# Attention's products cut into four products of 32 weight columns

## What is computed

```
Q = x @ Wq.T + bq ; K = x @ Wk.T + bk ; V = x @ Wv.T + bv      (heads of 8)
scores = einsum(Q, K) / sqrt(128), causal ; attn = softmax(scores)
x = layernorm(x + attn @ V @ Wo.T + bo)
w, i = top 2 of softmax(x @ gate_w.T), weights renormalised
x = layernorm(clip(x + w0 * expert_i0(x) + w1 * expert_i1(x)))
expert(x) = gelu(x @ w1 + b1) @ w2 + b2                        (128 -> 256 -> 128)
```

## Time and profile before

| what | value |
|---|---|
| median of 3 runs | 498.77 us (498.0 to 500.38) |
| profiled execution, span | 529.2 us |
| PE / weight loads / DVE / ACT / POOL busy | 84% / 53% / 74% / 62% / 52% |
| attention of one batch, steady | 40.3 us (from 142.3 to 182.6 us of the span) |
| in it: PE / DVE / ACT busy | 38.3 / 36.8 / 28.6 us |

### The profile page before, as it was taken

How to read it: one execution, slowest core, us unless ns; L and a number is a source line. 1 busy time by engine, 2 the same in 40 slices (tenths; PEclk the granted TensorE clock), 3 DMA queues, 4 the chain that set the end, 5 groups by cost and what they waited for, 6 DMA issues and landing times.

```text
span 529.2 us, 11188 instructions
## 1 busy us (share of the span) xinstructions
PE 442.3 (84%) x3577; PEld 279.2 (53%) x3610; DVE 389.1 (74%) x979; ACT 328.7 (62%) x810; POOL 275.6 (52%) x443
## 2 busy tenths in 40 slices
PE   8799999999999999999999898685687867776980
PEld 2355454454454454454454453264586866675970
DVE  7978889988989989989989998558444544442192
ACT  5285766776777776776776667456265766565045
POOL 6033234266456456456546557826655655656363
PEclk9999999999999999999999999989578898989896
DMA  6646595552542542452542311232333322221463
GB/s 179 194 150 185 162 279 162 159 152 82 169 152 83 171 151 77 147 178 77 159 138 87 102 52 30 74 83 78 103 108 97 82 71 69 69 63 32 144 215 119
DMA packets 74393, 64.60 MB, mean 122 GB/s; under 512 B 9030, under 2 KB 68685, under 8 KB 74336
## 3 DMA queue, kind: packets, MB, share of 16 engines
q1 hardware_dynamic: 68240, 55.01, 35.3%
q0 software_dynamic: 4512, 8.54, 5.0%
q10 hardware_dynamic: 1584, 0.34, 0.3%
HBM read 36.88 MB, written 25.46 MB: 118 GB/s over the span
## 4 chain that ended last, share of the span: by engine, by line
PE 47%; DVE 26%; issue 8%; ACT 7%; another core or an unknown queue 5%; DMA 3%; POOL 2%; ACTq 0%; SPq 0%; DVEq 0%; POOLq 0%
DVE nmax L1354 15%; PE psum L1022 9%; PE psum L1189 8%; PE psum L998 7%; PE psum L975 6%; PE psum L1206 6%; PE psum L983 3%; DMA experts<-o_dram 2%; DVE ov L1362 2%; PE psum L1043 2%; PE psum L1050 2%; PE psum L1181 2%; ACT probs L806 2%; PE psum L1082 1%
## 5 line engine op out<-in xcount | busy, mean ns | idle before, releaser
L806 ACT ACTIVATE probs<-psum 128x512 f32<-128x512 f32 x320 | 180.2, 596 | 85.2 <-PE psum L998 45.6
L1354 DVE TENSOR_REDUCE nmax<-psum 128x2 f32<-128x1024 f32 (+3 forms) x224 | 196.3, 911 | 23.7 <-PE psum L983 23.2
L689 POOL TENSOR_SCALAR_AFFINE_SELECT probs<-probs 128x512 f32<-128x512 f32 x186 | 85.0, 484 | 125.6 <-ACT probs L806 124.9
L975 PE MATMUL psum<-kst,qst 128*128 128x512 bf16 (+2 forms) x511 | 109.6, 300 | 6.4 <-DVE nmax L1354 5.6
L757 POOL DMA_INDIRECT o_dram<-probs,xs x77 | 76.8, 997 | 59.0 <-DVE probs L1583 34.0
L998 PE MATMUL psum<-qst,kst 128*128 128x128 bf16 (+3 forms) x480 | 102.0, 296 | 6.5 <-issue 2.9
L1022 PE MATMUL psum<-probs,vst 128*32 128x512 f32 (+3 forms) x1024 | 83.1, 442 | 0.1
L983 PE MATMUL psum<-bmask,bident 128*128 128x256 bf16 (+1 forms) x320 | 80.5, 251 | 0.1
L998 PEld LDWEIGHTS psum<-qst,kst 128*128 128x128 bf16 x512 | 40.4, 98 | 54.6 <-ACT probs L806 32.1
L975 PEld LDWEIGHTS psum<-kst,qst 128*128 128x128 bf16 x512 | 47.1, 98 | 32.9 <-DVE nmax L1354 12.3
L1189 PE MATMUL psum<-xsT,kst 128*128 128x128 f32 x148 | 27.3, 314 | 17.5 <-ACT hT_sb L919 11.5
(11 more groups left out here) (217 smaller groups left out, 709.8 us busy)
## 6 DMA issues: line engine op xcount, KB each, us to landing
kst<-dk SPq DMA_DIRECT2D x62, 128.0 KB, 3.0
qst<-dq SPq DMA_DIRECT2D x31, 256.0 KB, 3.1
xs<-xs_dram SPq DMA_DIRECT2D x77, 66.0 KB
experts<-o_dram SPq DMA_DIRECT2D x7, 512.0 KB, 4.4
dk<-k SPq DMA_DIRECT2D x7, 384.0 KB, 2.7
dq<-q SPq DMA_DIRECT2D x7, 384.0 KB
xT_sb<-in_xT SPq DMA_DIRECT2D x8, 256.0 KB
xTv_sb<-in_xT SPq DMA_DIRECT2D x8, 256.0 KB, 3.4
```

The source lines that it names most:

```text
L689: pool.affine_select(out=view, in_=view, compare_op=ALU.is_ge, fill=0.0, base=0, pattern=[[0, view.shape[1]], [1, P]], channel_multiplier= ...
L806: act.activation(probs[:, c % 2, p, kk * T:(kk + 1) * T], ps_t[:, k % 2, :], ACT.Exp, scale=SCALE).then_inc(S["exp_done"], 1)
L975: pe.matmul(bank[:, at:at + w], qst[:, c, e, P * i:P * i + P], kst[:, c, h, e, 0:w], start=(at == 0), stop=False, skip_group_check=True)
L1354: last = dve.tensor_reduce(o, i, AX.X, ALU.max, negate=True)
```

## The change

A helper `columns` issues a product as four narrow ones, each with 32 of the weight columns and 32 partitions of the output, with the same moving operand. It is used for the scores and their masks, the values, the output product and the ranks, and, from batch 1 on, for the projections and what is taken off them (`whole_or_columns`). The turning of the maxima becomes a single narrow product, since only 32 of the 128 columns of `nmq` were ever filled; `nmq` shrinks to 32 columns, and its clearing on DVE at the start goes. The ranks were one product with `tri` and ten of 14 columns with `ones`; now each of the four tiles of `hotb` is repeated over all the blocks behind it by a moving operand of stride 0, so that there are four products with `ones` (56, 42, 28 and 14 columns) beside that with `tri`, each of them cut in four.

```
-        nmq = sb("nmq", [P, 2, P], BF16)
+        nmq = sb("nmq", [P, 2, 32], BF16)
...
+            def columns(out, stationary, moving, **flags):
+
+                for g in range(4):
+                    last = pe.matmul(out[32 * g:32 * g + 32], stationary[:, 32 * g:32 * g + 32], moving,
+                                     skip_group_check=True, **flags)
+                return last
+
+            def whole_or_columns(b, out, stationary, moving, start):
+
+                if b == 0:
+                    return pe.matmul(out, stationary, moving, start=start, stop=True, skip_group_check=True)
+                return columns(out, stationary, moving, start=start, stop=True)
...
-                        pe.matmul(bank[:, at:at + w], qst[:, c, e, P * i:P * i + P], kst[:, c, h, e, 0:w],
-                                  start=(at == 0), stop=False, skip_group_check=True)
+                        columns(bank[:, at:at + w], qst[:, c, e, P * i:P * i + P], kst[:, c, h, e, 0:w],
+                                start=(at == 0), stop=False)
...
-                            last = pe.matmul(ps_t[:, k % 2, at % T:at % T + w],
-                                             kst[:, c, g % 2, pair, P * j:P * j + P],
-                                             qst[:, c, pair, P * j:T], start=True, stop=True, skip_group_check=True)
+                            last = columns(ps_t[:, k % 2, at % T:at % T + w],
+                                           kst[:, c, g % 2, pair, P * j:P * j + P],
+                                           qst[:, c, pair, P * j:T], start=True, stop=True)
...
-                pe.matmul(ps_o[:, 0:P], nmq[:, c % 2, :], bident[:], start=True,
+                pe.matmul(ps_o[0:32, 0:P], nmq[:, c % 2, :], bident[:], start=True,
...
-                        last = pe.matmul(halves[:, n, :], onT_sb[:, P * i:P * i + P], wo_sb[:], start=True, stop=True)
+                        last = columns(halves[:, n, :], onT_sb[:, P * i:P * i + P], wo_sb[:], start=True, stop=True)
...
-                    pe.matmul(ps_m[:, 0:EB], tri[:], hotb[:].rearrange("p i e -> p (i e)"), start=True, stop=False,
-                              skip_group_check=True)
+                    columns(ps_m[:, 0:EB], tri[:], hotb[:].rearrange("p i e -> p (i e)"), start=True, stop=False)
                     for i in range(NQ):
-                        for o in range(i + 1, NQ):
-                            pe.matmul(ps_m[:, E * o:E * o + E], ones[:], hotb[:, i, :], start=False, stop=False,
-                                      skip_group_check=True)
-                        last = pe.matmul(ps_m[:, EB:EB + E], ones[:], hotb[:, i, :], start=False, stop=(i == NQ - 1),
-                                         skip_group_check=True)
+
+                        behind = NQ - i
+                        last = columns(ps_m[:, E * (i + 1):EB + E].rearrange("p (n e) -> p n e", e=E), ones[:],
+                                       hotb[:, i:i + 1, :].to_broadcast([P, behind, E]), start=False,
+                                       stop=(i == NQ - 1))
```

More of the change, by code:

```diff
@@ L982, in score_unit @@
                         diag_blocks = bank.rearrange("p (n w) -> p n w", w=2 * P)[:, :, P:2 * P]
-                    pe.matmul(diag_blocks, bident[:], bmask[:, 0:diag_blocks.shape[1], :],
-                              start=False, stop=True, skip_group_check=True).then_inc(S["s_filled"], 1)
+                    columns(diag_blocks, bident[:], bmask[:, 0:diag_blocks.shape[1], :],
+                            start=False, stop=True).then_inc(S["s_filled"], 1)
             def score_bank(b, c, k):
@@ L997, in score_bank @@
                         if at // T == kk:
-                            last = pe.matmul(ps_t[:, k % 2, at % T:at % T + w],
-                                             kst[:, c, g % 2, pair, P * j:P * j + P],
-                                             qst[:, c, pair, P * j:T], start=True, stop=True, skip_group_check=True)
+                            last = columns(ps_t[:, k % 2, at % T:at % T + w],
+                                           kst[:, c, g % 2, pair, P * j:P * j + P],
+                                           qst[:, c, pair, P * j:T], start=True, stop=True)
                             if last_group(b, c):
-                                last = pe.matmul(ps_t[:, k % 2, at % T:at % T + P], bmask[:, 0, :], bident[:],
-                                                 start=False, stop=True, skip_group_check=True)
+                                last = columns(ps_t[:, k % 2, at % T:at % T + P], bmask[:, 0, :], bident[:],
+                                               start=False, stop=True)
                 last.then_inc(S["st_filled"], 1)
@@ L1042, in project @@
                 pe.wait_ge(S["xT_loaded"], 16 * (b + 1))
-                pe.matmul(bank, (wq_sb if name == "q" else wk_sb)[:], xT_sb[:], start=True, stop=True,
-                          skip_group_check=True).then_inc(filled[name], 1)
+                whole_or_columns(b, bank, (wq_sb if name == "q" else wk_sb)[:], xT_sb[:], True
+                                 ).then_inc(filled[name], 1)
             def take_off(b, name, n, bank):
@@ L1049, in take_off @@
                 pe.wait_ge(S[name + "_parts"], 3 * b + n)
-                pe.matmul(bank, nident[:], part[f"{name}_{n}"][:], start=False, stop=True, skip_group_check=True
-                          ).then_inc(S[name + "_left"], 1)
+                whole_or_columns(b, bank, nident[:], part[f"{name}_{n}"][:], False
+                                 ).then_inc(S[name + "_left"], 1)
             def shared(b, c, k, item, odd):
@@ L1073, in shared @@
                         i = n if item == "va" else n + 2
-                        last = pe.matmul(halves[:, n, :], xTv_sb[:, P * i:P * i + P], wv_sb[:], start=True, stop=True)
+                        last = columns(halves[:, n, :], xTv_sb[:, P * i:P * i + P], wv_sb[:], start=True, stop=True)
                 if item in ("woa", "wob"):
@@ L1300, in _ @@
                 dve.memset(kst[64 * h:64 * h + 64, :, 1 - h, :, :], 0.0).then_inc(S["st_zeroed"], 1)
-            dve.memset(nmq[:], 0.0)
             dve.memset(ones[:], 1.0).then_inc(S["const_ready"], 1)
```

## The result

The changed kernel took 493.62 us (median of 4 runs, 492.46 to 496.55) against 498.82 us for the kernel before (4 runs, 498.0 to 500.38): ratio 0.990, 95% interval 0.986 to 0.993. That is 5.2 us faster; 5.5 us were forecast, to 493.0.

A forecast was written before the change was run, and what follows sets the result against it. PE was taken to bound most of each attention batch, DVE some 15 us. Shape 9.5 plus ranks 0.8 minus hand-overs 2.5 gave 7.8 us; 2 given back left 5.8, scaled to 5.5: 493 us, range 484 to 503.

The forecast's parts named there:

- The shape: Around PE's blocks of probabilities times values: each costs 0.25 us beyond its work through shape changes, 16 us for 64 blocks.
- How often it counts: Blocks on the attention's chain of waits: six of eight a batch, so 1.5 us a batch, 12.0 us in eight.
- Four for one: PE's wide bf16 products cut in four narrow ones: no added time; upper bound 2.6 us a batch, 21 in all.
- floor rival: Quadruples of 128 columns on PE: least distance up to 0.11 us, 13 us slower, 512 us; chance 0.15.
- Ranks: Rank products on PE, eleven becoming five quadruples: 0.1 us less a batch, 0.8 in all.
- Hand-overs: Some sixteen a batch between PE and another engine on the chain: 0.02 us later each, 2.5 us in all.
- DVE's idle time: DVE in an attention batch: idle time falls from 3.5 to 2.5 us, its busy time staying at 36.8 us.
- The share given back to DVE: Places in the batch where DVE becomes the later engine: a quarter of the 7.8 us saved, 2 us, is lost again.
- The sum: Whole kernel: 7.8 us less, 2 given back, 5.8 against the profiled 529.2 us, scaled to 5.5 us, 493 us.
- Issue and fetching: PE's instruction packets growing from 30 to some 65: no cost expected, 5 us in all as upper bound.
- the sequencer: PE's front end becomes the bound if decoding exceeds 44 ns a product; at 60 ns about 615 us; chance 0.04.

The follow-up runs named there:

- wide maxima: Changed kernel with the single narrow product that turns the maxima put back to 128 columns: 551.2 us, 1.0435 against the kernel before.
- P.V stands at one place: Kernel before with both blocks of probabilities times values at k = 9, one behind the other, no added instruction: 546.69 us, ratio 1.0306.
- pieces experiment: Kernel before with score and mask products cut into pieces of 64 moving columns, all still wide, 7410 products instead of 2610: 565.68 us, ratio 1.0638.
- halves: Changed kernel with score products of 256 columns or more issued as two of half the columns, 10152 products: 581.72 us, 1.0937 against the kernel before.
- second profile of before: Kernel before run once more without edit for a trace: 531.34 us, beside a median of 529.24 us.
- light maxima: DVE's row maxima read half the columns: kernel before 513.36 us (0.9726); changed kernel 544.13 us (1.0259), and 547.24 us (1.0336) on another chip.

## Why the prediction was right, and what it missed

In the condition in which before takes 499 us, step by step:

- *The shape* was right. The start into a block is now its predecessor's own time (0.22 and 0.11 us, forecast 0.01 late or less); the blocks fell from 0.99 and 1.43 to 0.86 and 1.30 us. That is 0.13 on the way out, the 0.03 us of a bare load in it, since the load now runs ahead of the block. With 0.09 to 0.10 on the way in it is 0.22 to 0.23 us of the 0.25 a block. The wide maxima give 0.21 for another place.
- *How often it counts* was read from one batch, with six of eight blocks on the chain. In the batch behind it (182.6 to 223.2 us of the same profile) four are. So the 12.0 us of that term would have been 8 by the other batch.
- *Four for one* at no cost was right. A quadruple of 128 columns is 0.05 us from the next. A floor is there, but at 0.025 us for a quadruple (the ranks), far from the 0.075 from which the floor rival would have decided. The reading of the earlier trace rows had it right. The Trainium skill's page "TensorE: Matmul & The Clock Gate", section "Wait — 56ns, not 53.3ns?", puts the least distance of two starts at about 25 ns. This trace agrees for a whole quadruple (25 ns with 14 columns), but not for each of its products, of which four start within 10 ns.
- *Ranks* were mis-sized: 0.38 us saved a batch, 0.1 forecast, 3 us instead of 0.8 in eight batches. I had left room for a floor of 0.11 us a quadruple.
- *Hand-overs* (0.3 us a batch) were not measured by themselves.
- *DVE's idle time* was to be 2.5 us a batch and is 2.3; its wait for PE was to sink below 2 us and is 1.1; a batch was to take 39.4 to 39.8 and takes 39.4 to 39.6. The share given back to DVE is read from the chain (DVE's part in it doubled) and not shown by an experiment in this condition.
- *The sum* came out near, and that is in part luck. Steady batches shrank by 0.9 to 1.0 us, 7 to 8 us for eight, where the runs differ by 5.2; no profile of the kernel before in the first condition says where the rest went. Into the experts' stage the changed kernel is 12.2 us ahead of the profile of before (333.5 against 345.7 us on ACT), but these are profiles of two conditions. If, in the first condition, the kernel before takes as long as the changed one from that stage on, the whole 5.2 us lie in the attention, near the 5.8 of the sum; that is assumed and not shown. The 5.5 us were then got by scaling with a ratio of two conditions, which happened to change little. The prediction didn't speak of POOL's queue at all, which sets the end here.

In the second condition it was wrong, and the step that failed is *Issue and fetching*: "I take 0, and 5 us in all as upper bound". It goes with the rival *the sequencer*, which I gave 0.04 on the strength of one reading: 22 instructions passed within 0.2 us in the earlier trace rows, so a product "took 0.02 us at the most". That reading is true for a burst of 22 instructions and says nothing of what lasts: a batch with 928 products and 924 loads took 43.0 us, 0.046 us a product, and the rival's own point of decision was 44 ns a product. What the runs show in place of the 0 are halts without a semaphore that grow with the number of products, 11.5 to 12.9 us with 7080 against 0.4 with 2610 (2.2 where P.V stands at one place). That they arise in PE's front end fits them but is argued; the rival's 60 ns a product, and so its 615 us, did not come, nor is it a fixed time for each product, since within the bursts eight products start in 0.23 us. By added products the price is 7 ns in the pieces experiment (33.6 us for 4800, 2 ns of it the pieces' own time), 9 to 11 in the halves, and 5 to 7 for the change itself if the forecast 8 us of saved time are added back to the 16 to 22 lost ((16 + 8) / 4470 to (22 + 8) / 4470).

A second step failed silently. The prediction saw that the profiled execution was 6% longer than the median and turned it into a factor. By the profiles at hand those 30 us are not spread over the program: the experts' stage alone differs by as much between the conditions. A profile so far from the timed runs is of another regime, and the forecast should have said that its rows may not hold for the metric, or the reverse. Whether late instructions also make the experts' stage longer is open: the waits of the experts' stage of the kernel before are put down to "issue" as well (in the second profile of before, between 380 and 440 us, the loads of L1189 waited 19.6 us in 14 places, 3.8 at the longest), with only 715 products in 132 us.

What stays open is why the short halts come, and why in one condition only. The pieces experiment shows that the number of products brings them, and the light maxima that DVE then no longer sets the pace. The Trainium skill's page "Runtime: NRT & Kernel Launch", section "Instruction fetch mechanics", calls the crossing of a block of instructions mostly hidden. The profile in the first condition agrees: one halt of 1.2 us with 66 packets. The halves don't: nine long halts, 15.3 us together, each behind a packet's landing. For the short halts neither fetching nor decoding can be named as the cause. The recording of the profile is not: the timed runs lose as much as the profiled ones. Whether the sign in the first condition holds for other versions, as the halves or the pieces, could not be tried, as no chip of the experiments was in it.

## What to carry to other kernels

Alternating 128 and 32 weight columns costs 0.21 to 0.25 us for each pair of changes, and cutting wide bf16 products in four narrow ones costs nothing in array time; but count the instructions: at one product and one load every 43 ns (some 925 of each in 39.4 us) PE kept up in the first condition, and in the second it did not, on either chip on which the changed kernel was run. Test such a change on more than one chip, and don't scale a profile that is 6% off its timed runs: find first in which stage the difference lies. When the stage ahead gets faster, look at what queues behind it, here POOL's indirect writes at 1.28 us each. Read a term such as "six of eight blocks count" from more than one batch.

## What the hardware showed that was not expected

- The same two programs compare as 0.990 where the kernel before takes 499 us and as 1.033 to 1.045 where it takes 529 to 531, at the same granted clock of 1.00 in the attention.
- PE's loads stop for 0.7 us amid a quadruple (ahead of 129.84 us in the rows shown), only five products behind the halt before. The halts wait for no semaphore and come at the same places of the list: 24 of them and 11.5 us in the attention with 7080 products, 70 and 47.5 us with 10152, one of 0.4 us with 2610.
- All 13 halts of 0.8 us or more end 1.23 to 1.55 us behind the landing of a packet of instructions.
- Four narrow products to four column groups start within 0.01 us, and a quadruple of 14 columns takes 25 ns to the next, as much as one of 28.
- The experts' stage, the same instructions in both kernels, takes 105.0 us in one condition and 134.7 and 135.1 in the other, at a granted clock of 0.98 against 0.90 and 0.89.
